# Turning the rounded integers of the last stage by transposing DMAs instead of TensorE and a copy

## What is computed

```python
def _qdq(x):
    s = jnp.maximum(jnp.max(jnp.abs(x), axis=-1, keepdims=True) / 127.0, 1e-08)
    return jnp.clip(jnp.round(x / s), -127.0, 127.0) * s
...
o = jnp.einsum('bhnm,bmhd->bnhd', attn, v).reshape(B, N, C)
out = _qdq(o) @ _qdq(wp).T + bp
...
rms = jax.lax.rsqrt(jnp.mean(x * x, axis=-1, keepdims=True) + _NORM_EPS)
xn = x * rms * gamma
a_scale = 127.0 / (jnp.max(jnp.abs(xn), axis=-1, keepdims=True) + _EPS)
x_q = jnp.clip(jnp.round(xn * a_scale), -128.0, 127.0) / a_scale
...
x = x + jnp.tanh(g_xattn[1]) * _L1_xattn_ref(_layernorm(x, axis=-1), ctx_2048, ...)
x = x + jnp.tanh(g_ffn[1]) * _L1_ffn_ref(_layernorm(x, axis=-1), L1_ffn_gamma, L1_ffn_W)
```

## Time and profile before

| | us |
|---|---|
| median of 3 runs | 942.17 |
| lowest and highest | 941.64 and 942.39 |
| the profiled execution's own time | 938.89 |
| its span from first to last instruction | 937.2 |
| first `z_add` of the stage begins | 869.71 |
| last `z_add` begins | 932.56 |
| PE busy over the span | 801.4 (86%) |
| DVE busy | 757.8 (81%) |
| ACT busy | 573.3 (61%) |
| POOL busy | 553.1 (59%) |

### The profile page before, as it was taken

One profiled execution on the slowest core, in us unless ns is written; L12 is line 12 of the kernel. 1 busy time (PEld: TensorE's weight loads), 2 busy tenths in 40 slices (PEclk: granted clock), 3 DMA queues, 4 the chain that ended last, 5 costly groups with the idle time before them and its releaser, 6 DMA issues.

```text
span 937.2 us, 14453 instructions
## 1 busy us (share of the span) xinstructions
PE 801.4 (86%) x4253; PEld 349.0 (37%) x4253; DVE 757.8 (81%) x1510; ACT 573.3 (61%) x974; POOL 553.1 (59%) x604
## 2 busy tenths in 40 slices
PE   3798997789899999899999967799999999955663
PEld 3454453334344444444444432132323232222221
DVE  4999998788898899899888658587888888634884
ACT  4878887443566555566555544466666666646762
POOL 7856653133344444354443353699999999955661
PEclk9999999999999999999999987899999999997885
DMA  9987875523354242344333241313121311000111
GB/s 308 248 209 214 228 186 161 155 57 59 72 118 68 52 114 56 68 70 72 69 62 64 45 101 56 85 54 83 55 83 55 83 54 46 2 1 0 48 64 68
DMA packets 172394, 86.51 MB, mean 92 GB/s; under 512 B 124049, under 2 KB 156961, under 8 KB 172321
## 3 DMA queue, kind: packets, MB, share of 16 engines
q1 hardware_dynamic: 172000, 85.63, 36.8%
q10 hardware_dynamic: 320, 0.01, 0.0%
HBM read 37.76 MB, written 12.58 MB: 54 GB/s over the span
## 4 chain that ended last, share of the span: by engine, by line
PE 34%; DVE 23%; issue 10%; ACT 6%; SPq 4%; POOL 3%; DMA 1%; DVEq 0%; ACTq 0%; POOLq 0%
PE bank L1116 10%; PE bank L1128 5%; PE bank L1208 4%; PE bank L1198 3%; PE bank L1179 3%; SPq L435 3%; POOL B L663 3%; DVE bank L1543 3%; DVE gsm L1545 3%; DVE B L1554 3%; DVE B L1548 2%; PE bank L1326 2%; ACT bank L817 2%; DVE B L1669 2%; ACT A L944 1%
## 5 line engine op out<-in xcount | busy, mean ns | idle before, releaser
L1116 PE MATMUL bank<-A,B 128*128 128x512 f16 x1024 | 232.4, 380 | 13.2 <-DVE B L1554 13.1
L1669 DVE TENSOR_REDUCE B<-bank 128x1 f32<-128x512 f32 x256 | 161.7, 682 | 53.1 <-PE bank L1179 53.0
L594 POOL TENSOR_TENSOR B<-B 128x512 f16<-128x512 f32 x64 | 75.7, 1183 | 215.4 <-DVE B L1554 132.2
L944 ACT ACTIVATE A<-bank 128x512 f32<-128x512 f32 x256 | 142.7, 602 | 90.0 <-PE bank L1198 86.5
L663 POOL TENSOR_TENSOR B<-B,A 128x512 f32<-128x512 f32 x124 | 160.0, 1325 | 0.5 <-ACT A L944 0.5
L1116 PEld LDWEIGHTS bank<-A,B 128*128 128x128 f16 x1024 | 99.1, 98 | 138.6 <-DVE B L1554 16.4
L1128 PE MATMUL bank<-A,B 128*128 128x512 f16 x512 | 120.7, 379 | 0.0
L817 ACT ACTIVATE bank<-B 128x512 f32<-128x512 f32 x64 | 38.5, 602 | 130.4 <-DVE B L1548 130.4
L1179 PE MATMUL bank<-A 96*128 96x512 f16 x256 | 99.7, 405 | 12.2 <-DMA A<-B 4.8
L1198 PE MATMUL bank<-A 98*128 98x512 f16 x256 | 96.6, 389 | 14.9 <-ACT A L944 7.3
L663 POOL TENSOR_TENSOR B<-A 128x512 f32<-128x512 f32 x64 | 79.9, 1270 | 20.8 <-ACT A L944 20.5
(11 more groups left out here) (215 smaller groups left out, 1462.0 us busy)
## 6 DMA issues: line engine op xcount, KB each, us to landing
B<-in_L_ffn_w_dram SPq DMA_DIRECT2D x48, 256.0 KB, 3.5
A<-k_parts SPq DMA_DIRECT2D x48, 128.0 KB, 2.5
A<-B SPq DMA_DIRECT2D x192, 32.0 KB, 1.9
X<-in_x_dram SPq DMA_DIRECT2D x4, 1024.0 KB, 8.8
B<-in_ctx_dram SPq DMA_DIRECT2D x16, 256.0 KB, 5.3
k_parts<-B SPq DMA_DIRECT2D x16, 256.0 KB, 4.3
v_rows<-B SPq DMA_DIRECT2D x16, 256.0 KB, 2.5
B<-v_rows SPq DMA_DIRECT2D x16, 256.0 KB, 3.2
```

The lines of the kernel that those rows point to most:

```text
L594: nc.gpsimd.tensor_tensor(HLb[j][:, 1, :], Db[j % 2], HLb[j][:, 0, :], ALU.subtract).then_inc(lo_done, 1)
L944: nc.scalar.activation(PR[(HG * t + j) % 8], bank[2 + j % 2][:, :], ACT.Exp, scale=SCALE).then_inc(exp_done, 1)
L1116: last = mm(bank[2 * n + q][:, :], XQT[a][:, m, :], wt[:, m % DB, j * 512:j * 512 + 512], start=(m == 0), stop=(m == 2 * DB - 1))
L1669: reduce(NMX[g % 2][:, t, j:j + 1], bank[ROW_BANKS[r % 3]][:, :], AX.X, ALU.max, negate=True).then_inc(row_max, 1)
```

## The change

Both turns become transposing DMAs issued by SyncE (`turn_o`, `turn_z`), from OI to OIT and from ZI to ZT. TensorE's `turn_pair` and ACT's two copies go. SyncE's list for step s is the turn of O for unit s+1, the turn of Z for unit s-2, the store of unit s-3. ACT rounds O two units ahead (s+2) and itself makes the integers ZI right after rounding Z; DVE's `z_ints` goes, and its `o_ints` runs for unit s+1. TensorE runs project O of unit s first, then project Z of unit s-3.

```diff
+            def turn_o(u):
+
+                sp.wait_ge(oi_ready, u + 1)
+                up_to(sp, w_ps, u)
+                sp.dma_start_transpose(OIT, both(OI)).then_inc(oit_in, 16)
+
+            def turn_z(u):
+
+                sp.wait_ge(zi_ready, u + 1)
+                up_to(sp, z_ps, u)
+                sp.dma_start_transpose(ZT, both(ZI)).then_inc(zt_in, 16)
...
+            turn_o(0)
+            for s in range(UNITS + LAG):
+                if s + 1 < UNITS:
+                    turn_o(s + 1)
+                if 0 <= s - 2 < UNITS:
+                    turn_z(s - 2)
+                if 0 <= s - LAG < UNITS:
+                    store(s - LAG)
...
-                if live(s - 3):
-                    act.wait_ge(zi_ps, s - 2)
-                    up_to(act, z_ps, s - 3)
-                    nc.scalar.copy(ZT.rearrange("p n t -> p (n t)"), bank16[5]).then_inc(zt_out, 1)
-                if live(s):
-                    act.wait_ge(oi_ps, s + 1)
-                    up_to(act, w_ps, s)
-                    nc.scalar.copy(OIT.rearrange("p n t -> p (n t)"), bank16[4]).then_inc(oit_out, 1)
-                if live(s + 1):
-                    o_round(s + 1)
+                if live(s + 2):
+                    o_round(s + 2)
                 if live(s - 2):
                     act.wait_ge(zs_ready, s - 1)
                     for t in range(2):
                         last = nc.scalar.activation(Z[:, t, :], Z[:, t, :], ACT.Copy, bias=RND, scale=ZR[:, t:t + 1])
                     last.then_inc(z_rounded, 1)
+                    act.wait_ge(z_rounded, s - 1)
+                    up_to(act, zt_in, 16 * (s - 2))
+                    nc.scalar.activation(ZI, Z, ACT.Copy, bias=-RND).then_inc(zi_ready, 1)
...
             def out_step(s, live):
+                if live(s):
+                    pe.wait_ge(oit_in, (s + 1) * 16)
+                    up_to(pe, ro_ready, s)
+                    project(0, OIT, WPT, w_ps)
                 if live(s - 3):
                     u = s - 3
-                    pe.wait_ge(zi_ready, u + 1)
-                    up_to(pe, zt_out, u)
-                    turn_pair(bank16[5], ZI, zi_ps)
-                if live(s):
-                    pe.wait_ge(oi_ready, s + 1)
-                    up_to(pe, oit_out, s)
-                    turn_pair(bank16[4], OI, oi_ps)
-                if live(s - 3):
-                    pe.wait_ge(zt_out, u + 1)
+                    pe.wait_ge(zt_in, (u + 1) * 16)
                     up_to(pe, z_added, u)
                     project(2, ZT, WLT, z_ps)
-                if live(s):
-                    pe.wait_ge(oit_out, s + 1)
-                    up_to(pe, ro_ready, s)
-                    project(0, OIT, WPT, w_ps)
...
             def o_ints(u):
                 dve.wait_ge(o_rounded, u + 1)
-                up_to(dve, oi_ps, u)
+                up_to(dve, oit_in, 16 * u)
...
                 if live(s - 2):
                     z_stats(s - 2)
-                if live(s - 3):
-                    z_ints(s - 3)
-                if live(s):
-                    o_ints(s)
+                if live(s + 1):
+                    o_ints(s + 1)
```

More of the change, by code:

```diff
@@ L253, in flamingo_kernel @@
         o_ps, s_ps, den_ready, o_norm = sem("o_ps"), sem("s_ps"), sem("den_ready"), sem("o_norm")
-        osc_ready, o_rounded, oi_ready, oi_ps, oit_out = sem("osc_ready"), sem("o_rounded"), sem("oi_ready"), sem("oi_ps"), sem("oit_out")
+        osc_ready, o_rounded, oi_ready, oit_in = sem("osc_ready"), sem("o_rounded"), sem("oi_ready"), sem("oit_in")
         w_ps, ro_ready, ro_scaled, x3_ready, st4, f_ready = sem("w_ps"), sem("ro_ready"), sem("ro_scaled"), sem("x3_ready"), sem("st4"), sem("f_ready")
-        zs_ready, z_rounded, zi_ready, zi_ps, zt_out = sem("zs_ready"), sem("z_rounded"), sem("zi_ready"), sem("zi_ps"), sem("zt_out")
+        zs_ready, z_rounded, zi_ready, zt_in = sem("zs_ready"), sem("z_rounded"), sem("zi_ready"), sem("zt_in")
         z_ps, z_added, centred = sem("z_ps"), sem("z_added"), sem("centred")
@@ L495, in _, with store @@
             batches(sp, feed)
[L497 to L503, removed]
+            both = lambda a: a.rearrange("p t d -> p (t d)")
+            def turn_o(u):
[6 more added lines that the diff above has]
+                sp.dma_start_transpose(ZT, both(ZI)).then_inc(zt_in, 16)
+            def store(u):
+                sp.wait_ge(z_added, u + 1)
+                sp.dma_start(out_rows[:, bass.ds(u * 2, 2), :], X[:, bass.ds(u * 2, 2), :]).then_inc(out_done, 16)
+            turn_o(0)
[6 more added lines that the diff above has]
+                    store(s - LAG)
             sp.wait_ge(out_done, 16 * UNITS)
@@ L996, in out_step @@
                     last.then_inc(z_rounded, 1)
+                    act.wait_ge(z_rounded, s - 1)
+                    up_to(act, zt_in, 16 * (s - 2))
+                    nc.scalar.activation(ZI, Z, ACT.Copy, bias=-RND).then_inc(zi_ready, 1)
             act.wait_ge(osc_ready, 1)
             o_round(0)
+            o_round(1)
             for s in range(UNITS + LAG):
@@ L1315, in _ @@
             pe.wait_ge(o_norm, DB * BATCH)
[L1317 to L1321, removed]
             def project(first_bank, src, wt, done):
@@ L1793, in z_scales @@
                 last_.then_inc(zs_ready, 1)
[L1795 to L1798, removed]
             def z_add(u):
@@ L1819, in out_step @@
                     link(ts(ZSC, ZAM, LSC, None, ALU.mult))
+            o_ints(0)
             for s in range(UNITS + LAG):
```

## The result

| | before | the change |
|---|---|---|
| median | 942.0 us | 944.45 us |
| ratio to before | | 1.0032, 95% interval 1.0020 to 1.0045 |
| profiled execution: span | 937.2 us | 944.7 us |
| o_ints(0) begins | 841.53 | 845.92 |
| **start**: from there to the first `z_add` | 28.18 | 32.77 |

The change is slower by 0.32%, 3.0 us, and its interval does not reach 1; the forecast was 3.1 us. (The two medians themselves differ by 2.45 us.) The two profiled executions differ by 7.5 us, but 4.4 of these lie ahead of o_ints(0), in code that is the same in both kernels. Executions of the kernel before scatter by about as much: 937.3 to 943.2 us, without one of its twenty, which took 1793.6 us. So the stage has to be compared from its own beginning: 98.78 against 95.67 us, which is 3.11 us more.

What follows compares the result with a forecast made beforehand. The last stage was taken as bound by a DVE and ACT loop of 8.35 us a step plus 0.6 for a late project Z. Start 2.9 plus steps 0.2 made 3.1 us more, 945.3 us by the median, range 941.5 to 948.7.

Steps and rivals of the forecast that it cites:

- The start: Last stage, from o_ints(0) to the first `z_add`: bare turns and single buffers were to cost 2.9 us, bounds 1.2 to 4.6.
- the steps: Seven steps from first to last `z_add`: 63.1 us against 62.85, 0.2 us more, bounds -0.5 to +1.9.
- The bound of 4.6: Upper bound of the start's cost in us, if project O(3) and project Z(0) are both slow.
- The formula of two steps: Path from one `z_add` to that of two units later; O 3.60, Z 1.90 gives 17.81 us, 8.90 a step.
- The 0.85 us for a pair of two slow projects: In the steps: one pair of three with half a chance of both projects slow, 1.7/2 = 0.85 us.
- the floor of 8.64 us: Least time per step: the loop DVE, ACT, DVE with ZI on ACT, from the end of `zs_ready`, 8.64 us.
- full clock: Faster rival: both projects at full clock from the start, steps at the floor, 3.95 us less, 938.2; chance 0.12.
- Late landings or pairs of two slow projects: Much slower rivals: each pair slow, +10, 952 us; or each landing at 5.4, +17, 959 us; chance 0.08 together.
- Slow start only: Rival of no change: start +2.9 us, then steps at the floor, 60.5 us, -2.35; total 942.7; chance 0.18.
- the expected gain: Last stage: `z_add` waits 10.5 us for PE, late project Z 0.6 us a step; forecast as not gained.

Runs made afterwards that it cites:

- Run 4: The change with two buffers each for OI and OIT and TensorE's loop written out: start 29.97 instead of 32.77 us, ratio to the kernel before 0.9999.
- run 11: The change with two buffers each for OI and OIT, unit 0 of O turned by TensorE and copied by ACT: start 29.33 us, ratio to before 0.9997.
- run 6: The change with extra unused matmuls, 16 before project O(0), 12 after project Z of each step but the last: ratio to before 0.9988.
- run 1: The kernel before with Z alone turned by DMA, its integers made by ACT: ratio to before 1.0011 (0.9994 to 1.0027).
- run 9: The kernel before with extra unused matmuls: 8 before the first turn, 4 per step with a project O, 12 in each of the last two: ratio 0.9933.
- run 10: The change with rounded O written by ACT to two free banks and read there by `o_ints` in two operations: ratio to before 1.0050.
- run 5: The kernel before with 4 extra unused matmuls ahead of the turns in each step that has a project O: ratio 0.9979.

## Why the prediction was right

Its total, 3.1 us more, was met: 3.0 by the ratio, 3.11 in the stage. That it was met so closely is luck: its two terms were each 1.7 us off, in opposite directions. The start came out at the upper end of its own bounds (4.6), the steps, at -1.5, beyond the lower end of theirs (-0.5). What was not luck is the direction and the order of waits.

The start was to cost 2.9 us and cost 4.59. Point by point, in us after the beginning of o_ints(0):

| | predicted | measured |
|---|---|---|
| project O(0) begins | 3.89 | 3.98 |
| `z_stats`(0) | 13.91 | 14.30 |
| `o_ints`(3), released by the landing | 17.47 | 17.73 |
| `z_scales`(0) | 18.17 | 19.66 |
| project O(3), behind ZI and RO | 25.52 | 26.88 |
| project Z(0) | 29.12 | 30.25 |
| first `z_add` | 31.07 | 32.77 |

The mechanism was right in each line: the bare landings, the two single buffers, `z_scales` queued behind `o_ints`(3), project O ahead of project Z. Run 4, which takes the single buffers away, and run 11, which takes the first landing away, gave 2.8 and 0.6 us back. Mis-sized was one duration: I gave `o_ints`(3) 0.7 us, from rows in which it never ran beside POOL's multiplication, and it took 2.01. That is 1.3 of the 1.7 us. Having moved an operation in time, I should have looked at what it would now run beside. Project Z(0) at 2.49 instead of 1.90 adds 0.6, and 0.2 is won back elsewhere, net of a landing that came 0.3 later. The bound of 4.6 was drawn up for another reason, O(3) and Z(0) both slow.

The steps were to cost 0.2 us and gained 1.5. (7 x 8.90 + 0.85 is 63.15, so the sum should have read 0.3.) The formula of two steps, 12.31 plus both projects, with one slow and one fast, gave 17.81 us; measured were 17.54, 17.35 and 18.04. With TensorE's 3.27 us from the start of project O to that of project Z, and 2.03 for Z, the first comes out at 12.31 + 3.27 + 2.03 = 17.6. The 0.85 us for a pair of two slow projects did not come. Of the rest, the three pairs were 0.5 us shorter together than drawn up, and the last step, 8.42 us, was 0.5 us shorter than its 8.90. The size of this term was wrong, and so was the floor of 8.64 us, which measured 8.41.

Of the smaller statements, removing `z_ints` from DVE freed nothing, as said; `z_scales` now waits 0.86 to 0.93 us for the centring in the middle steps, instead of 0.26. Landings were 3.1 us. The new operation on ACT took 1.06 instead of 1.05. Project O was released by ACT's RO in the steps and project Z stood right behind it; `z_add` waited 10.1 us for PE, where "about 10" was said.

The rivals: full clock did not come by itself, and run 6 shows part of what it would have needed. Late landings or pairs of two slow projects did not come. "Slow start only" had the steps at 60.5, and the 61.35 measured is nearer to that than to the forecast's 63.1; its start, taken as 2.9 us, was as much too small as the forecast's. The Trainium skill's advice ("VectorE: DVE Perf Modes", section "Rules for kernel authors"), TensorE's way for a 128x128 transpose where a result in PSUM will do, holds here for O at the start, where it won 0.6 us (run 11), but for Z the DMA costs nothing (run 1): what decides is whether the landing has something beside it.

**Where did the expected gain go?** The change takes two turns (1.14 us together), two copies (1.01 and 1.02) and `z_ints` (0.69) out of a middle step, 3.9 us of busy time on three engines, and puts 1.06 us on ACT. In a step that DVE and ACT fill, none of this was on the path. In a step that ends late it was, for Z, as these rows of the kernel before show, which lead to the project Z of 893.50:

```profile
890.94 0.69 DVE L1798 TENSOR_SCALAR B<-B 128x1024 f16<-128x1024 f32 x1
...
891.77 1.33 PE L1320 MATMUL bank<-id,B 128*128 128x128 f16 x16 [3.00 <-DVE B L1798]
...
892.43 1.01 ACT L985 COPY B<-bank 128x1024 f16<-128x1024 f16 x1
```

But what came in their place, RO and a slow project O, or the landing, is as long, and the step still ends with a project that runs at the lower clock after TensorE's gap. With less work on TensorE the gap does not get smaller.

## What to carry to other kernels

- A turn by DMA lands after 3.1 us whatever TensorE's way costs; it is free where a unit of work lies beside it and bare in the first units. There second buffers were worth 2.8 us, about as much as the whole change lost.
- When an operation is moved, look at what it will run beside. A fast `tensor_scalar` on DVE from SBUF to SBUF beside a long GpSimd operation went from 0.69 to 2.58 us.
- In a tail bound by a chain of waits, removing work from TensorE is worth nothing if its projects then run at half clock. Extra matmuls whose result nothing uses took 0.67% off the kernel before (run 9), where the change added 0.32%.

## What the runs showed of the hardware that I had not expected

- **DVE and GpSimd block each other.** `o_ints`, 128x1024 from SBUF to SBUF, took 0.69 us alone and 1.13, 2.01 and 2.58 us when GpSimd's multiplication of 2.35 us had begun before it; each time it ended 0.55 to 0.56 us after the multiplication. Read from a bank, twice 128x512, it took 1.28 to 1.29 in all cases (run 10). GpSimd's operations beside it stretch too, the `pow` from 0.71 to 1.09 us.
- **Extra matmuls are paid back by the granted clock.** In run 5 project Z, 8 matmuls, took 1.90 us in each of five cases in which 4 extra matmuls had ended 1.5 to 2.3 us before it. In run 9 it took 1.90 in five of eight units and 2.59 to 3.60 in the three others, two of which had 4 extra matmuls ahead, so 4 of them are not always enough. The granted clock of the whole span rose from 0.954 in the profiled execution of the kernel before to 0.969 in run 9.
